# Key projections of the third and fourth batch one and two quarters later, and the norm of x1 in two halves in every stage

## Time and profile before

| | us |
|---|---|
| median of 3 runs | 502.23 (499.87 to 503.01) |
| profiled execution | 501.24 |
| its span on the core | 499.0 |
| TensorE matmul busy | 441.0 (88%) |
| VectorE busy | 379.9 (76%) |
| ScalarE busy | 287.5 (58%) |
| POOL busy | 227.7 (46%) |
| mean granted clock of TensorE | 0.977 |

### The profile page before, as it was taken

The page is one execution under the profiler, slowest core; times in us unless marked ns, Lnnn a source line. Parts: engine busy times, 40 slices in busy tenths (PEclk is TensorE's granted clock), DMA queues, the critical chain, the costliest instruction groups (busy, mean ns, idle before and its releaser), DMA issues.

```text
span 499.0 us, 6242 instructions
## 1 busy us (share of the span) xinstructions
PE 441.0 (88%) x1919; PEld 187.6 (38%) x1919; DVE 379.9 (76%) x638; ACT 287.5 (58%) x513; POOL 227.7 (46%) x226
## 2 busy tenths in 40 slices
PE   8999888898988899899889898998999897988994
PEld 3433434233332224363342323544433332324563
DVE  4888997967669898487798898798658689644285
ACT  4244362344466666644777766646786545687443
POOL 5568797542158995341589785434022011020000
PEclk9999998999989989999999999998999989999999
DMA  6746464233396522223954204220243210000101
GB/s 204 264 143 179 132 190 116 68 81 75 99 242 177 129 64 72 79 75 105 240 130 121 73 2 116 76 75 2 64 106 76 74 55 1 2 0 1 43 1 43
DMA packets 26512, 47.33 MB, mean 95 GB/s; under 512 B 5456, under 2 KB 16368, under 8 KB 26480
## 3 DMA queue, kind: packets, MB, share of 16 engines
q1 hardware_dynamic: 24512, 44.05, 33.2%
q10 hardware_dynamic: 1968, 2.88, 2.1%
HBM read 35.19 MB, written 9.96 MB: 90 GB/s over the span
## 4 chain that ended last, share of the span: by engine, by line
PE 58%; DVE 24%; ACT 7%; issue 5%; POOL 3%; ACTq 1%; DMA 0%; DVEq 0%; POOLq 0%
PE bank L657 16%; DVE MX L1655 11%; PE bank L671 10%; PE bank L732 8%; PE bank L718 6%; PE bank L709 6%; DVE W L1556 3%; ACT PT L1230 3%; PE bank L822 3%; PE bank L689 2%; POOL W L1985 2%; DVE st L1529 1%; PE bank L948 1%; PE bank L859 1%; PE bank L842 1%
## 5 line engine op out<-in xcount | busy, mean ns | idle before, releaser
L1655 DVE TENSOR_REDUCE MX<-bank 128x1 f32<-128x512 f32 x256 | 166.0, 682 | 72.7 <-PE bank L709 68.5
L1230 ACT ACTIVATE PT<-bank 128x512 f32<-128x512 f32 x256 | 145.1, 597 | 86.7 <-PE bank L718 81.8
L709 PE MATMUL bank<-KS,QS 96*128 96x512 bf16 x240 | 89.5, 391 | 22.0 <-DVE MX L1655 21.0
L718 PE MATMUL bank<-QS,KS 99*128 99x512 bf16 x256 | 96.4, 390 | 8.5 <-ACT PT L1230 7.2
L732 PE MATMUL bank<-PT,Vs 128*32 128x512 f32 x512 | 70.9, 626 | 4.5 <-ACT PT L1230 4.3
L1985 POOL TENSOR_TENSOR W<-qT,W 128x512 f32<-128x512 f32 x48 | 63.2, 1320 | 19.9 <-DVE W L1556 8.7
L718 PEld LDWEIGHTS bank<-QS,KS 99*128 99x128 bf16 x256 | 24.4, 98 | 98.9 <-issue 59.0
L709 PEld LDWEIGHTS bank<-KS,QS 96*128 96x128 bf16 x240 | 23.6, 99 | 69.1 <-DVE MX L1655 45.8
L1974 POOL TENSOR_TENSOR W<-kT,W 128x512 f32<-128x512 f32 x32 | 41.7, 1302 | 6.7 <-ACT kT L1080 6.7
L1556 DVE TENSOR_TENSOR_SCAN W<-bank,W 128x512 f32<-128x512 f32 x32 | 38.8, 1212 | 0.2 <-ACT bank L1095 0.2
L1800 DVE TENSOR_TENSOR_SCAN W<-bank,W 128x512 f32<-128x512 f32 x32 | 38.2, 1211 | 0.4 <-DVE oS L1819 0.2
(11 more groups left out here) (228 smaller groups left out, 725.1 us busy)
## 6 DMA issues: line engine op xcount, KB each, us to landing
W<-v_rows SPq DMA_DIRECT2D x20, 512.0 KB, 9.9
k_parts<-parts SPq DMA_DIRECT2D x24, 128.0 KB, 2.3
KS<-k_parts SPq DMA_DIRECT2D x16, 192.0 KB, 3.5
q_parts<-parts SPq DMA_DIRECT2D x24, 128.0 KB, 2.4
QS<-q_parts SPq DMA_DIRECT2D x16, 192.0 KB, 3.5
cT<-in_cT SPq DMA_DIRECT2D x4, 512.0 KB, 4.0
xtok<-in_x SPq DMA_DIRECT2D x4, 512.0 KB, 9.9
W<-v_rows ACTq DMA_DIRECT2D x4, 512.0 KB, 5.9
```

The source lines that it names most:

```text
L709: pe.matmul(bank(n, b)[:, :], QS[0:NS, h, i * P:(i + 1) * P], KS[0:NS, h, :], start=True, stop=True).then_inc(filled(n, b), 1)
L718: pe.matmul(bank(name, b)[:, :], KS[0:NR, h, kt * P:(kt + 1) * P], QS[0:NR, h, :], start=True, stop=True).then_inc(filled(name, b), 1)
L1230: act.activation(PT[:, n % 2, j, :], bank(name, b)[:, :], ACT.Exp).then_inc(emptied(name, b), 1)
L1655: dve.tensor_reduce(MX[:, NT * h + i:NT * h + i + 1], bank(n, b)[:, :], AX.X, ALU.max).then_inc(emptied(n, b), 1)
```

## The change

For the third and fourth batch (`o` in stages 1 and 2) K0 moves from quarter (1, 2) to (1, 3) and K1 from (1, 3) to (2, 1). What is made of them moves too: the copies and the first part on ScalarE from (2, 0) to (2, 2), the rest on VectorE from (2, 3) to (3, 0), the second part from (3, 0) to (3, 1), the third on POOL from (3, 1) to (3, 2). The tables are changed to match; each use keeps its bank and its number. The norm of x1, in halves at (5, 3) and (6, 0) for the second batch already, is so for the third and fourth as well. No instruction is added or taken away.

```diff
--- before.py
+++ after.py
@@ -49,7 +49,7 @@
 
 
 SIDE_USES = {
-    (0, 0): ("V0", "b", 1), (0, 1): ("V1", "b", 2), (1, 2): ("K0", "o", 2), (1, 3): ("K1", "o", 1),
+    (0, 0): ("V0", "b", 1), (0, 1): ("V1", "b", 2), (1, 3): ("K0", "o", 2), (2, 1): ("K1", "o", 1),
     (2, 0): ("var", "o", 0), (2, 3): ("y0", "f", 2), (3, 0): ("y1", "f", 1), (3, 2): ("gv0", "r", 0),
     (4, 0): ("gy0", "o", 2), (4, 1): ("gy1", "o", 1), (4, 2): ("gv1", "r", 0),
     (5, 0): ("gg", "r", 2), (5, 1): ("gq", "r", 0), (5, 2): ("gk", "r", 1), (5, 3): ("t0", "f", 2),
@@ -59,8 +59,8 @@
 }
 
 
-FIRST_USES = {**{at: use for at, use in SIDE_USES.items() if use[0] not in ("gt0", "gt1", "Q0", "Q1") and use[1] != "f"},
-              (6, 2): ("gt0", "o", 1), (6, 3): ("gt1", "o", 2), (7, 1): ("Q0", "o", 0), (7, 2): ("Q1", "o", 1)}
+FIRST_USES = {**{at: use for at, use in SIDE_USES.items() if use[0] not in ("K0", "K1", "gt0", "gt1", "Q0", "Q1") and use[1] != "f"},
+              (1, 2): ("K0", "o", 2), (1, 3): ("K1", "o", 1), (6, 2): ("gt0", "o", 1), (6, 3): ("gt1", "o", 2), (7, 1): ("Q0", "o", 0), (7, 2): ("Q1", "o", 1)}
 
 THIRD_USES = {**{at: use for at, use in SIDE_USES.items() if use[0] not in ("gt0", "gt1", "Q0", "Q1")},
               (6, 2): ("gt0", "o", 1), (6, 3): ("gt1", "o", 2), (7, 1): ("Q0", "o", 0), (7, 2): ("Q1", "o", 1)}
@@ -761,11 +761,11 @@
                     pe.wait_ge(o_sq, count(1, o, 1))
                     pe.wait_ge(*free_for("var", o))
                     project(bank("var")[:, :], lambda k: mavg[:, :], lambda k: sq[:, k, :]).then_inc(filled("var"), 1)
-                if at == (1, 2):
+                if at == ((1, 2) if o == 1 else (1, 3)):
                     pe.wait_ge(w2_in, W2_ALL)
                     pe.wait_ge(cT_in, count(16, o, 16))
                     by_feature("K0", o, xwk, 0, cT)
-                if at == (1, 3):
+                if at == ((1, 3) if o == 1 else (2, 1)):
                     by_feature("K1", o, xwk, 1, cT)
                 if at == (4, 0):
                     pe.wait_ge(gated, count(1, o, 1))
@@ -1144,7 +1144,7 @@
                 if o == 1:
                     second_batch(at)
                     return
-                if at == (2, 0):
+                if at == (2, 2):
                     for m in range(ND):
                         act.wait_ge(*full_of(f"K{m}", o))
                         act.wait_ge(v_out, count(16, o, 16))
@@ -1154,7 +1154,7 @@
                     act.wait_ge(*read("K1", o))
                     act.wait_ge(Q_out, count(96, o, 0))
                     act.activation(parts[:, 0, :, :], full32[:, :, :], ACT.Copy).then_inc(K_hi, 1)
-                if at == (3, 0):
+                if at == (3, 1):
                     act.wait_ge(K_r1, count(1, o, 1))
                     act.activation(parts[:, 1, :, :], full32[:, :, :], ACT.Copy).then_inc(K_mid, 1)
                 if at in (((7, 1), (7, 2)) if o == 2 else ((7, 2), (7, 3))):
@@ -1567,7 +1567,7 @@
                     ins = dve.scalar_tensor_tensor(ab[:, m, :], kz[:, m, :], 0.0, ab[:, m, :], ALU.min, ALU.subtract)
                     if m == 2:
                         ins.then_inc(z_ls, 1)
-                if at == (2, 3) and o > 1:
+                if at == (3, 0) and o > 1:
                     first_rest(K_hi, K_r1, o)
                 if at == (7, 3) and o == 2 or at == (8, 0) and o == 3:
                     first_rest(Q_hi, Q_r1, o)
@@ -1582,10 +1582,7 @@
                 if at in ((4, 3), (5, 1)):
                     dve.wait_ge(*read(f"gy{at[0] - 4}", o))
                     statistics(0, xtok, o, at[0] - 4)
-                if o > 1 and at == (5, 3):
-                    dve.wait_ge(x2_done, count(NT, o - 1, 0))
-                    norm(0, xtok, x1b[:, o % 2, :, :], x1_done, o)
-                if o == 1 and at in ((5, 3), (6, 0)):
+                if at in ((5, 3), (6, 0)):
                     dve.wait_ge(x2_done, count(NT, o - 1, 0))
                     norm(0, xtok, x1b[:, o % 2, :, :], x1_done, o, ((0, 1), (2, 3))[at[0] - 5])
 
@@ -1997,7 +1994,7 @@
                     pool.wait_ge(o_gate, count(1, o, 1))
                     pool.tensor_tensor(oS[:, :, :], oS[:, :, :], rsd.unsqueeze(1).broadcast_to([P, ND, S]),
                                        ALU.mult).then_inc(gated, 1)
-                if at == (3, 1) and o > 1:
+                if at == (3, 2) and o > 1:
                     second_rest(K_mid, K_lo, o)
                 if at == (5, 2):
                     inverse_deviation(0, o)
```

## The result

| | before | after |
|---|---|---|
| median, us | 501.69 (499.87 to 504.27, 8 runs) | 498.50 (496.49 to 500.71, 8 runs) |
| profiled execution, us | 501.24 | 498.83 |
| its span, us | 499.0 | 496.5 |
| mean granted clock in it | 0.977 | 0.983 |

The ratio is 0.9923, interval 0.9896 to 0.9950: 3.9 us less by the ratio, 3.2 us by the medians. It is inside the 1% that counts as no change and 0.1 us under the low end of the range. The ratios leave out runs more than 1.5% above the fastest of their kernel (three of the norm alone, four of before); medians and means count all runs. Two more measurements of the same kernel, 12 runs each, are among the experiments: 0.9963 (0.9923 to 1.0003) and 0.9949 (0.9916 to 0.9982).

The account below looks back on a forecast made before the run. TensorE was taken as the bound (busy 441.0 of 499.0 us), VectorE where it holds TensorE. Stage 1 -0.8 and stage 2 about -0.2 (+0.45 - 0.6) gave -1.0 us, from 502.23 to 501.2 us; range 498.6 to 504.4.

Parts of the forecast that it names:

- K0 one quarter on, the wait replaced by one for ScalarE: Stage 1: score tile (1, 3) waits for ScalarE's exponential instead; of 1.62 us only the maximum's 0.22 us is saved.
- Score tile (2, 2): Starts at 210.52 us in stage 1, 0.82 us ahead, and at 319.2 in stage 2, 0.3 ahead.
- The next wait doesn't take it back: Stage 1 behind score tile (2, 2): TensorE stays 0.8 us ahead, and nothing but TensorE bounds up to 237 us.
- The subtraction: L1499 on VectorE, now behind two maxima and the addition of y0, takes 1.23 us with POOL's product over.
- rival (b): Slower: the moved subtraction on VectorE keeps its 2.2 us; sum +0.55 us, 502.8 us; chance 20%.
- VectorE later in stage 2: VectorE ends the subtraction at 325.2 us, 0.45 us later; score tile (3, 3) starts at 326.9 instead of 326.57.
- The norm in halves: Norm of x1, stage 2: bank free 0.6 us sooner, TensorE's 2.13 us stop becomes 1.55; -0.6 us.
- The sum: Stage 1 -0.8 us and stage 2 -0.2 us give -1.0 us, median 501.2 us; chance 40%.
- Rival (a): The slow stretch of TensorE's clock behind the 2.13 us stop goes: -1.0 - 1.7, 499.5 us; chance 23%.
- The low end of the range: 498.6 us: 499.5 us less 1 us, since the three runs shown lie 3.1 us apart.

Follow-up runs that it names:

- the norm alone: Only the norm of x1 in halves, on the kernel before, measured twice: 501.38 us, ratio 0.9984, and 500.84 us, ratio 0.9984.
- with fillers: Idle matmuls at five stops of TensorE, on the changed kernel: 498.30 us, ratio 0.9929; with the rest of K also back at (2, 3): 497.02 us, 0.9903.
- the rest one quarter earlier: Changed kernel with the rest of K on VectorE back at quarter (2, 3): 499.62 us, ratio 0.9940.
- the filler alone: Kernel before plus six idle matmuls in TensorE's 2.13 us stop of stage 2, norm in one piece: 502.44 us, ratio 0.9995.
- the late rest: Changed kernel with two unused reductions of 0.6 us each on VectorE ahead of the rest of K, both stages: 500.91 us, ratio 0.9967.
- the kernel before with fillers: Kernel before plus idle matmuls at five of TensorE's longest stops: 498.43 us, ratio 0.9938.

## Why the prediction came out as it did

- **K0 one quarter on, the wait replaced by one for ScalarE: right.** The score tile started at 202.88 (202.60 forecast, 202.86 with the offset) and at 311.25 (311.3), and K0 had no wait. All nine traces of moved keys stop there 1.50 us in stage 1.
- **Score tile (2, 2): right.** 211.00 against 210.78, and 319.24 against 319.2. Between slots 0 and 6 stage 1 gave 0.52 to 0.73 us in the six traces of moved keys without additions there (forecast 0.8), and 0 and 0.14 with fillers, where K0 waits again.
- **The next wait doesn't take it back: nearly right.** Nothing did up to 241 us, but 0.28 us of it went between slots 10 and 12, where TensorE stands 0.2 us ahead of a maximum tile ("issue", so perhaps for a transfer) in the trace of the change and in one other of the six.
- **The subtraction: right.** 1.22 us twice, where rival (b) had 2.2. The rule of the Trainium skill ("GPSIMD Engine Reference", "Key points"), that GpSimd and VectorE share interfaces to SBUF, agrees with the three durations before and with 1.22 us at the old place as soon as POOL was through (trace of the rest one quarter earlier).
- **VectorE later in stage 2: right for VectorE, too large for TensorE.** VectorE was through with the subtraction 0.36 us later (325.08 against 324.72; forecast 0.45). TensorE lost less: 0 by slot 4 and 0.24 by slot 6. Score tile (3, 3) came at 326.70, not at 326.9.
- **The norm in halves: right on the wait.** 1.48 us (1.55 forecast). The step from slot 6 to 8 is 1.8 us with the halves and 1.4 with the filler, which shortens no wait: that leaves 0.4 for the halves, not 0.6.
- **The sum, and the choice to leave the clock out of it: wrong.** The steps add to -1.0 us; 0.5 was found step by step in the trace, and 1.0 at full clock in the runs. What failed is the term for TensorE's clock, which the sum put at nothing. Rival (a) had it and was the case that came; it was given 23% against 40% for the sum without it, and it was taken for a single stretch of 1.7 us. What the runs showed in its place: a mean time at low clock 3.7 us shorter (error 1.3; 4.6 over all runs), worth 1.3 to 1.8 us. The stretch at 343 us is gone from the trace and from every other with the halves, and the one at 459 us is missing as well, far behind all that was moved; the second is not explained and can be luck. The profile had the evidence: of the stops read for the prediction the longest had a stretch behind it, and those of stage 1, 1.62 us and less, had none.
- **The low end of the range.** Rival (a) at 499.5 less 1 us is 498.5, and the range says 498.6; the measured median is 498.50. That it fell just outside says little; that the gain was 3.9 us by the first ratio, and 2.7 us in the mean of the 24 later runs, where 1.0 was forecast says more. The first eight runs were also the fastest of the three measurements of the changed kernel (medians 498.50, 500.46 and 498.78 us); part of their distance to the forecast may be luck in the clock.

What remains open: why a stretch far behind an edit comes or goes. One trace shows one execution, and the stretches lie otherwise in each: the first in the three traces of the changed kernel starts at 77.1, 113.9 and 77.7 us. The kernel before and the one with the late rest have the stretch at 459 us, the other 12 traces not. Nor is it shown why the filler alone left the mean time at low clock at 22.3 us, with 23.1 in before beside it. That less idle time, by the halves or by a filler, takes a stretch away is shown for one place, by two traces against twelve, and the times of the norm alone bear it out only weakly; a sum over the whole kernel could not be made from these runs.

## What to carry to other kernels

When a change shortens a stop of TensorE, look at the granted clock behind the stop first: a stretch at half clock that follows it can be worth more than the stop (here 1.4 us against 0.4). Put it into the sum as a term of its own, with a chance, since the same stop has a stretch behind it in some executions only, and take its size from the mean over many runs (span and clock of each) and not from one trace. Before an operation on VectorE is moved, see what POOL does beside it at the new place and at the old one.

## What the runs showed of the hardware

- The same f32 subtraction of 128 x 1024 on VectorE takes 1.22 us with POOL idle and 2.12 to 2.26 us beside a product of two inputs of that size on POOL, which loses nothing by it (2.35 us, 2.37 alone).
- A stretch at 1.2 GHz lasts 3.4 us (29 of them in the 14 traces) or 6.8 us (8), and the one at the end of each trace 4.3 to 7.5 us. At the norm of stage 2 it comes behind a stop of 2.13 us (2 traces) and not behind one of 1.48 us, or a filler of 1.46 and a stop of 0.84. At K0 in stage 1 it came at stops of 1.71 and 2.09 us and not at 2.58. At a stop of 2.0 to 2.4 us near 77 us it came in 5 of 11 traces.
- Matmuls that do nothing, 28 beside 1,919, bring the time at low clock from 22.8 to 11.0 us and the kernel's from 502.7 to 499.1 us (means of one group).
- The granted clock explains much of the spread of the runs: 0.36 us of span for each us at low clock, in a kernel whose 105 runs lie from 497.4 to 506.8 us.
- Where K0 waits for the context in stage 1, the transfer takes from issue to use 4.0 us in one execution and 4.1 to 4.5 us in four others (issued 196.35, K0 at 200.88 in the kernel before with fillers): a wait behind it varies by half a us without any edit to the transfer.
